# Shared experts on float16 parts, with the routed experts gathered into one stretch ahead of the last two chunks

## The reference, cut to what matters

```
logits = x @ gate_w.T                         # 32 experts in 8 groups, 3 groups kept, 6 experts per token
slot   = flat_e * 48 + pos                    # at most 48 slots per expert, the first tokens win
xb     = buf[:E * C].reshape(E, C, h)         # the slots' tokens
g, u   = split(xb @ w_gate_up)                # per expert, 176 + 176 columns
yb     = (silu(g) * u) @ w_down
out    = sum over the token's 6 slots of topk_w * yb
gs, us = split(x @ ws_gate_up)                # shared experts: all tokens, 352 + 352 columns
out    = out + (silu(gs) * us) @ ws_down
```

## Time and profile before

| what | us |
|---|---|
| median of 3 runs | 1727.3 (1720.38 to 1727.62) |
| the profiled execution | 1723.16 |
| its span, first to last instruction | 1721.3 |
| PE busy | 1472.5 (86%) |
| DVE busy | 1140.3 (66%) |
| ACT busy | 732.4 (43%) |
| POOL busy | 239.7 (14%) |
| mean granted clock of TensorE | 0.935 of full |

### The profile page before, as it was taken

How to read it: one execution, slowest core, us unless ns; L and a number is a source line. 1 busy time by engine, 2 the same in 40 slices (tenths; PEclk the granted TensorE clock), 3 DMA queues, 4 the chain that set the end, 5 groups by cost and what they waited for, 6 DMA issues and landing times.

```text
span 1721.3 us, 25882 instructions
## 1 busy us (share of the span) xinstructions
PE 1472.5 (86%) x9746; PEld 824.6 (48%) x9747; DVE 1140.3 (66%) x2283; ACT 732.4 (43%) x1232; POOL 239.7 (14%) x249
## 2 busy tenths in 40 slices
PE   4999999967989986568888898888988888998897
PEld 2666666644548876223344443343533344433355
DVE  5666666647421124688938779859879678789475
ACT  5455555511212220416755126754137752157630
POOL 3344444411330000100010000110000110000000
PEclk8999999987999988659999999999999998999998
DMA  2000000006014421232102012211023101113000
GB/s 112 14 26 25 24 24 24 24 13 195 15 40 128 151 76 63 64 61 44 32 10 40 1 37 44 44 28 34 1 44 56 44 19 25 34 27 45 31 1 25
DMA packets 137484, 75.23 MB, mean 44 GB/s; under 512 B 117648, under 2 KB 126352, under 8 KB 136592
## 3 DMA queue, kind: packets, MB, share of 16 engines
q1 hardware_dynamic: 136800, 72.02, 17.2%
q0 software_dynamic: 576, 1.77, 0.4%
HBM read 37.59 MB, written 9.06 MB: 27 GB/s over the span
## 4 chain that ended last, share of the span: by engine, by line
issue 57%; POOL 3%; DVE 0%; POOLq 0%; DVEq 0%
POOL rs_sb L1446 1%; POOL xs_sb L1452 1%; POOL ve_sb L1443 0%; POOL qks_sb L1466 0%; DVE bn_sb L1623 0%; DVE x_sb_sb L1656 0%; POOL v_sb L1464 0%; POOL qks_sb L1456 0%; POOLq L66 0%; POOLq L1159 0%; DVE mv_sb L1629 0%; DVEq L1159 0%; POOL v_sb L1463 0%; POOL qks_sb L1467 0%; DVE ident_h_sb L1839 0%
## 5 line engine op out<-in xcount | busy, mean ns | idle before, releaser
L1526 ACT ACTIVATE room_sb<-s_ps 128x1024 f32<-128x1024 f32 (+1 forms) x320 | 293.1, 940 | 176.1 <-PE s_ps L1998 172.2
L1707 DVE TENSOR_REDUCE mx_sb<-s_ps 128x1 f32<-128x512 f32 (+1 forms) x400 | 249.5, 650 | 60.3 <-PE s_ps L1974 37.7
L1971 PE MATMUL s_ps<-room_sb 48*128 48x512 f16 (+3 forms) x480 | 145.6, 340 | 33.8 <-DVE mx_sb L1702 21.3
L2018 PE MATMUL cm_ps<-room_sb,v_sb 128*32 128x512 f32 (+3 forms) x1536 | 157.0, 496 | 1.0 <-ACT room_sb L1532 0.8
L1998 PE MATMUL s_ps<-room_sb 51*128 51x128 f16 (+4 forms) x1152 | 136.6, 273 | 11.3 <-ACT room_sb L1526 7.9
L2124 PE MATMUL cm_ps<-w_fd_sb,room_sb 128*128 128x256 f32 x512 | 132.8, 409 | 12.6 <-DVE room_sb L1785 12.6
L1443 POOL TENSOR_TENSOR ve_sb<-mv_sb,eps_sb 128x4 f32<-128x4 f32 x24 | 5.3, 220 | 896.5 <-DVE mv_sb L1629 841.9
L396 DVE SCALAR_TENSOR_TENSOR x_sb_sb<-xp_sb,conv_w_sb,x_sb_sb 128x512 f32<-128x512 f32 x96 | 106.8, 1115 | 22.6 <-ACT x_sb_sb L319 20.5
L1971 PEld LDWEIGHTS s_ps<-room_sb 48*128 48x128 f16 x480 | 41.7, 94 | 155.2 <-DVE mx_sb L1707 79.4
L2124 PEld LDWEIGHTS cm_ps<-w_fd_sb,room_sb 128*128 128x128 f32 x512 | 98.3, 200 | 36.7 <-issue 14.0
L2111 PE MATMUL s_ps<-xbT_sb,w_fg_sb 128*128 128x512 f16 x384 | 102.0, 396 | 8.4 <-DVE ctok_sb L1755 7.7
(11 more groups left out here) (265 smaller groups left out, 2953.6 us busy)
## 6 DMA issues: line engine op xcount, KB each, us to landing
we_gu_sb<-we_gu SPq DMA_DIRECT2D x32, 352.0 KB
we_dn_sb<-we_dn SPq DMA_DIRECT2D x32, 176.0 KB
x_in_sb<-x SPq DMA_DIRECT2D x9, 512.0 KB, 3.6
rows<-x_sb_sb SPq DMA_DIRECT2D x8, 512.0 KB, 3.0
x_sb_sb<-rows SPq DMA_DIRECT2D x2, 2048.0 KB, 11.5
out<-x_sb_sb SPq DMA_DIRECT2D x8, 512.0 KB, 2.9
room_sb<-qks_sb SPq DMA_TRANSPOSE x88, 3.3
xp_sb<-w_in SPq DMA_DIRECT2D x1, 1024.0 KB, 5.5
```

What stands on the lines that cost most here:

```text
L1526: act.activation(weights[(g * NU + u) % SLOTS_P][:, 2 * pair:2 * pair + 2, 0:width(u) * P], W[s % 2][:, :, 0:width(u) * P], ACT.Exp, scale ...
L1707: dve.tensor_reduce(mx[:, pair, k % 2, slot:slot + 1], max_bank(g, m)[:, 0:count * P], AX.X, ALU.max, negate=True).then_inc(mx_ok, 1)
L1971: last = pe.matmul(bank[:, at * P:(at + plain) * P], query[head:head + NORM, i * P:(i + 1) * P], key[head:head + NORM, j * P:(j + plain) * ...
L2018: last = pe.matmul(O[32 * h:32 * h + 32, (i - half * GT) * P:(i - half * GT + count) * P], v[:, j, g * HG + h, :], weights[(g * NU + u) % ...
```

## The change

Five things, all of them in the first two parts of the program:

1. `conv_mlp_phase` splits the transposed result into two float16 parts, a high one by ACT from PSUM and a low one by POOL (which had copied float32). It also loads the shared experts' weights, on SP's queue in step 1, and splits them into two float16 parts in the last two steps. `experts_phase` then waits for no constants before its first chunk.
2. Each float32 product of the shared experts becomes three float16 products (high by high, low by high, high by low). The product of silu and up is made by DVE in all groups, in place, and split by ACT (high) and by POOL (low, groups 0 to 2) or DVE (low, from group 3).
3. A round is chunks 0 to 2, the four tiles of the group before, chunks 3 to 5. DVE's shared products are written in between the steps of the routing.
4. Counting moves to round 3, the slots' transposes to the last three turns of round 6 (eight in each), `gather` behind `add(3)`; all 32 experts stand in the first eight turns of round 7, four in each. The transposes of the slots' outputs follow, two in each of the two chunks and four tiles left, on two PSUM banks instead of four.
5. The slots' outputs and the one-hot matrices of the combination become float16 parts (they were float32r).

```diff
 # conv_mlp_phase
+                if n.reg is None and n.off == 1:
+                    for dst, src in zip(got_shared, ("ws_gu", "ws_dn")):
+                        sp.dma_start(dst[:], io[src]).then_inc(shared_ld, 16)
...
-                    wait(pool, xaT_ok, c(1, 1))
-                    pool.tensor_copy(xT[:, :, bass.ds(c(GTOK), GTOK)], xaT[:, :, :]).then_inc(xT_ok, 1)
+                    wait(pool, xTh_ok, c(1, 1))
+                    own = bass.ds(c(GTOK), GTOK)
+                    pool.tensor_tensor(xT[1][:, :, own], xaT[:, :, :], xT[0][:, :, own], ALU.subtract).then_inc(xT_ok, 1)
...
                     act.activation(xaT[:, :, :], tp[:, :, :], ACT.Copy).then_inc(xaT_ok, 1)
+                    act.activation(xT[0][:, :, bass.ds(c3(GTOK), GTOK)], tp[:, :, :], ACT.Copy).then_inc(xTh_ok, 1)
...
                     if has_c:
-                        wait(pe, xaT_ok, c3(1, 1))
+                        wait(pe, xTh_ok, c3(1, 1))
 # experts_phase
-COUNT_AT = 2
+COUNT_AT = 3
...
-SLOTS_AT = 5
-MOE_AT = 6
+SLOTS_AT = 6
+MOE_AT = 7
...
+EARLY = 3
+LATE = EARLY + GT
+TURNS = GT + 2 * NSX
+MOE_TURNS = LATE + 1
...
-        y = [sb(f"y{i}", [P, CJ, D], F32R) for i in range(2)]
+        y = [sb(f"y{i}", [P, CJ, D], F16) for i in range(2)]
...
         def experts_at(g, i):
-            n = (g - MOE_AT) * (GT + 2 * NSX) + i
-            return range(n * E // MOE_SLOTS, (n + 1) * E // MOE_SLOTS) if g >= MOE_AT else range(0)
+            return range(i * E // MOE_TURNS, (i + 1) * E // MOE_TURNS) if g == MOE_AT and i < MOE_TURNS else range(0)
+        def slots_at(g, i):
+            return range(8 * (i - LATE), 8 * (i - LATE) + 8) if g == SLOTS_AT and i >= LATE else range(0)
+        def outputs_at(g, i):
+            if g == MOE_AT:
+                return range(2 * (i - MOE_TURNS), 2 * (i - MOE_TURNS) + 2) if i >= MOE_TURNS else range(0)
+            return range(4 + 2 * (i - EARLY), 6 + 2 * (i - EARLY)) if g == NG else range(0)
+        def turns(g):
+            for i in range(TURNS):
+                chunk, tile = (i, None) if i < EARLY else (None, i - EARLY) if i < LATE else (i - GT, None)
+                if (chunk is not None and g < NG) or (tile is not None and g > 0):
+                    yield i, chunk, tile
 # POOL
             for g in range(1, NG):
                 if g < DVE_AT:
-                    act(g)
+                    act_low(g)
+                add(g - 1)
                 if g == GATHER_AT:
                     gather()
-                add(g - 1)
 # DVE
+            def product(g, i):
+                wait(dve, sg_ok, NSX * g + i + 1)
+                wait(dve, gu_mm, 2 * NSX * g + 2 * i + 2)
+                dve.scalar_tensor_tensor(sg[:, i, :], mm[(2 * i + 1) % 4][:, :], 1 / W_SCALE, sg[:, i, :],
+                                         ALU.mult, ALU.mult).then_inc(sa_ok, 1)
+            def low(g, i):
+                if g >= DVE_AT:
+                    wait(dve, sh_ok, NSX * g + i + 1)
+                    wait(dve, dn_mm, 2 * g)
+                    dve.tensor_tensor(su[1][:, i, :], sg[:, i, :], su[0][:, i, :], ALU.subtract).then_inc(sl_ok, 1)
+            product(0, 0)
             dve.memset(gm[:, :, EG:], LOW)
...
+            low(3, 0)
+            product(3, 1)
             dve.wait_ge(cnt_ok, 2)
             for i in range(2):
                 last = dve.max_index(at8[i][:, :], needle[:, i * (CJ - 8):i * (CJ - 8) + 8], cum[:, :])
+                if i == 0:
+                    low(3, 1)
+                    product(3, 2)
             last.then_inc(cnt_ok, 1)
+            low(3, 2)
+            product(4, 0)
 # PE
                 for k in range(KD):
-                    last = pe.matmul(mm[c % 4][:, :], ws_gu[:, k, col:col + P],
-                                     xT[:, k, g * GTOK:(g + 1) * GTOK], start=(k == 0), stop=(k == KD - 1))
+                    for wp, xp in PRODUCTS:
+                        last = pe.matmul(mm[c % 4][:, :], ws_gu[wp][:, k, col:col + P],
+                                         xT[xp][:, k, g * GTOK:(g + 1) * GTOK],
+                                         start=(k == 0 and wp == xp), stop=(k == KD - 1 and xp == 1))
...
             def down(g, t):
                 if t == 0:
-                    wait(pe, sa_ok, NSX * (g + 1))
+                    wait(pe, sl_ok, NSX * (g + 1))
...
-            pe.wait_ge(consts, 16 * N2)
...
+            def slot_out(j):
+                if j == 0:
+                    pe.wait_ge(ey_ok, E)
+                wait(pe, y_ok, j - 1)
                 for k in range(KD):
-                    last = pe.transpose(mm[j % 4][:, k * P:(k + 1) * P],
+                    last = pe.transpose(tp[j % 2][:, k * P:(k + 1) * P],
...
+            for g in range(NG + 1):
+                for i, c, t in turns(g):
+                    if c is not None:
+                        gate_up(g, c)
+                    if t is not None:
+                        down(g - 1, t)
...
+                        slot_features(m)
+                    experts(g, i)
+                    if (g, i) == (MOE_AT, MOE_TURNS - 1):
+                        expert_down(E - 1)
+                    for j in outputs_at(g, i):
+                        slot_out(j)
+                    if g == COUNT_AT and t == GT - 1:
+                        counted()
 # combination
-        hot = [sb(f"hot{i}", [P, CJ, P], F32R) for i in range(QUAD)]
+        hot = [sb(f"hot{i}", [P, CJ, P], F16) for i in range(QUAD)]
```

More of the change, by code:

```diff
@@ L355, in _ @@
                     squares(x1, ss2, ss2_ok)
+                if n.reg is None and n.off == NG:
+                    act.wait_ge(shared_ld, 32)
+                    for src, dst in zip(got_shared, shared):
+                        act.activation(dst[0][:, :, :], src[:, :, :], ACT.Copy, scale=W_SCALE).then_inc(wa_ok, 1)
         @block.vector
@@ L421, in _ @@
                     convolve(2)
+                if n.reg is None and n.off == NG + 1:
+                    for i, (src, dst) in enumerate(zip(got_shared, shared)):
+                        dve.wait_ge(wa_ok, 6 + i)
+                        dve.scalar_tensor_tensor(dst[1][:, :, :], src[:, :, :], W_SCALE, dst[0][:, :, :],
+                                                 ALU.mult, ALU.subtract).then_inc(wv_ok, 1)
+                    dve.wait_ge(wv_ok, 7)
                 if has_c:
@@ L831, in _ @@
             then(last)
+            product(0, 2)
             then(dve.memset(t8[:, :, TOPG:], LOW))
             for t in range(NT):
+                if t == NT // 2:
+                    product(1, 0)
                 last = dve.match_replace(gr[:, t, :], t8[:, t, :], gm[:, t, :], TAKEN)
@@ L845, in _ @@
             then(last)
-            dve.tensor_tensor(ex, sc[:, :, 0:E], t8b[:, :, 0:1].to_broadcast([P, NT, E]), ALU.subtract).then_inc(sub_ok, 1)
+            product(1, 2)
+            then(dve.tensor_tensor(ex, sc[:, :, 0:E], t8b[:, :, 0:1].to_broadcast([P, NT, E]), ALU.subtract))
+            assert step[0] == CENTERED
             then(dve.memset(t8b[:, :, TOPK:], LOW))
             for t in range(NT):
+                if t == NT // 2:
+                    product(2, 0)
                 last = dve.match_replace(sr[:, t, :], t8b[:, t, :], sc[:, t, :], TAKEN)
@@ L971, in down @@
                 if t == 0:
-                    wait(pe, sa_ok, NSX * (g + 1))
+                    wait(pe, sl_ok, NSX * (g + 1))
                     wait(pe, so_ok, 2 * g)
                 for k in range(NSX):
-                    last = pe.matmul(ro[t // 2][:, t % 2, :], su[:, k, t * P:(t + 1) * P], ws_dn[:, k, :],
-                                     start=(k == 0), stop=(k == NSX - 1))
+                    for ap, wp in PRODUCTS:
+                        last = pe.matmul(ro[t // 2][:, t % 2, :], su[ap][:, k, t * P:(t + 1) * P], ws_dn[wp][:, k, :],
+                                         start=(k == 0 and ap == wp), stop=(k == NSX - 1 and wp == 1))
                 if t % 2:
@@ L1011, in counted @@
             def counted():
+                pe.wait_ge(consts, 16 * N2)
                 pe.wait_ge(pre_ok, 8)
@@ L1053, in _ @@
                 last.then_inc(ty_ok, 1)
+            for g in range(NG + 1):
+                for i, c, t in turns(g):
+                    if c is not None:
+                        gate_up(g, c)
+                    if t is not None:
+                        down(g - 1, t)
+                    if g == SLOTS_AT and t == 0:
+                        pe.wait_ge(cnt_ok, 1)
+                        pe.wait_ge(cum_ok, NG)
+                        pe.matmul(tp[0][0:1, 0:NT], ones_f[:, 0:1], busy_f[:, :], start=True, stop=True).then_inc(busy_mm, 1)
+                    for m in slots_at(g, i):
+                        if m == 0:
+                            pe.wait_ge(busy_ok, 1)
+                            pe.wait_ge(gath, 16 * CJ)
+                        slot_features(m)
+                    experts(g, i)
+                    if (g, i) == (MOE_AT, MOE_TURNS - 1):
```

(9 more changed lines are left out.)

204 lines of the change are left out of this document (87 added, 117 removed).

## The result

| | before | after |
|---|---|---|
| median of 4 runs each, us | 1726.27 (1720.38 to 1727.62) | 1768.73 (1765.23 to 1773.32) |
| ratio, 95% interval | | 1.0256 [1.023, 1.0282] |
| profiled execution / its span, us | 1723.16 / 1721.3 | 1769.33 / 1767.5 |
| mean granted clock | 0.935 | 0.895 |
| PE busy, us | 1472.5 | 1502.0 |

What follows compares the result with a forecast made beforehand. PE, 95% busy in the routed experts, and its granted clock were taken to bound the kernel. 1723.2 + 40 (experts' block) - 2 (combination) = 1761 us, stated as 1759 for possible clock recoveries; range 1734 to 1775.

Steps and rivals of the forecast that it cites:

- rival A: The forecast itself: the low clock holds through the routed experts, four in a row; 1759 us, range 1745 to 1773; 74%.
- Rival D: Low clock as in rival A, but DVE's waits for chunks start the experts 10 to 15 us later; 1772 us; 5%.
- outputs to the block's end: Transposes of the slots' outputs behind the experts: 19 us, 14 at the full clock; block ends at 681 us.
- combination: Behind the experts' block, 192 products at 0.109 us, each quad waiting for one-hot matrices: between -5 and 0, taken as -2 us.
- The clock: In the experts' stretch: four experts in a row without shared work bring the granted clock to 0.5.
- The length: Experts' stretch: 4.5 us per expert at the low clock, 1.55 more than at full; 158 us, 156 with a full-clock start.
- The page that spoke the other way: Trainium skill's rule against long idle gaps between matmul bursts: half-microsecond gaps among the experts would keep the full clock.
- Rival B: The clock holds at the full level through four experts in a row; experts end at 604.5, total 1699 us; 12%.
- First part: `conv_mlp_phase`: ACT's extra copy and POOL's subtraction cost up to 0.2 us in seven steps, 1 us in all, within 0 to 7.
- Slots: Three turns with eight slot transposes each before the experts: 15 us, bounds 11 and 19; experts begin at 506.
- Routing: DVE's chain with shared products between its steps: starts at 401.9, casts end at 449.4, index at 465 us.
- a sign of being wrong: Experts beginning much before 495 or after 520 us, or a clock of 0.9 or more in their stretch.

Runs made afterwards that it cites:

- the kernel with the bank of its own: The kernel after, with the experts' second products in a PSUM bank of their own, so first products no longer wait for ACT's copy: 1725.75 us, ratio 1.0039.
- the last version: The kernel after with a bank for second products, two wide products per following expert, one before 22 slot transposes, POOL's additions of groups 2 to 6 held back: 1693.52 us.

## Why the prediction was right, step by step

The forecast came true in direction and range: 1768.7 us, slower, in 1734 to 1775. The mechanism is the one that rival A named, the low clock through the experts. The time itself lies 10 us above A's 1759 and 3 below D's 1772, since the start was late as D had it. The main size, 159 us for 156, came out of two errors that cancel. Most other terms came out longer than the prediction had them.

| step | predicted | measured | off by |
|---|---|---|---|
| chunk / tile at the full clock, start to start, us | 1.30 / 0.98 | 1.30 / 0.99 | |
| first chunk, at | 396 | 399.7 | +3.7 |
| index, at | 465 | 469.5 | +4.5 |
| down(3) ends, at | 467.5 | 472.3 | +4.8 |
| slots' turns begin, at | 491 | 497.3 | +6.3 |
| experts' first turn, at | 506 | 517.25 | +11.3 |
| an expert at the low clock, us | 4.5 | 4.77 | +0.27 |
| experts' stretch, from that turn's chunk, us | 156 | 159 | +3 |
| outputs to the block's end, us | 19 | 17.7 | -1.3 |
| combination, us | -2 | -3.6 | -1.6 |

- *The clock.* Right in level. That the order is enough for it, the run of the kernel before in rows of four shows; whether it is all of it is open, since the kernel after with its experts spread, most of them still in pairs, got 0.63 only. My reason for it, that PE did little but expert products, was half of it: narrow products, put into the waits, hold the clock too, and why they do is open.
- *The length.* An expert cost 4.77 us at the low level, not 4.5; by the prediction's own sum that makes 166.5 us of the stretch, not 158. The clock came back twice for some 3.2 us, which gave 6.5 back, and 159 is what was left. That these two nearly cancel is luck. The price of the low level was mis-sized twice: the two experts of the earlier trace rows lie 2.83 us apart (its rows do not show the 2.97), so it is 4.77 - 2.83 = 1.94 us for each expert and not 1.55.
- *The page that spoke the other way.* Rival B rested on full clock through gaps of half a microsecond. The gaps did matter (filled, they give B's clock in most executions, and a stretch of 92.6 us where B had 99.5), but they are short, and that section of the Trainium skill ("TensorE: Matmul & The Clock Gate", "Why this matters for your kernels") warns of long ones. The measurement decides: 0.52 with gaps of 0.51 us, and a fall at 584.5 us with no gap at all in the kernel with the bank of its own.
- *First part.* Six of the seven steps cost nothing: from one normalization to the next 42.36 us after, 42.34 before. The last one, beside which the weights are split, took 1.5 us more (43.10 against 41.58). The first normalization stands 3.07 us later (92.46 against 89.39 us), ahead of any step; another execution with the same first part has it at 88.46 and its first chunk at 395.94, as forecast. So most of the 3.7 us is one execution's start, not the change.
- *Slots.* Predicted 15 us with bounds of 11 and 19, measured 19.9. Mis-sized for two reasons: the low part that waits beside POOL's addition (1.74 us, in which PE stood idle for DVE), and a clock that fell there already, at 501.5 us; the next two chunks took 2.4 to 2.8 us. The fall came behind this wait, but without the addition it came too.
- *Routing.* The index came 0.8 us later than the late start explains. The prefix sums took 7.05 us, where they had taken 5 x 0.69 and I had counted no change. POOL's additions account for 2.0 us of that (5.03 without them); the rest stands beside POOL's low part, which no run took away.
- *Rival D.* The start was 10 to 15 us late as D had it, but for another reason than the counting of DVE's waits that D gave: start-up, POOL beside DVE and the early fall of the clock. The first expert began at 519.81 us, just inside the 520 that the prediction had named as a sign of being wrong.

The sum by the profile: 693.9 - 640.6 = 53.3 us at the block's end, 3.6 us back in the combination, and 3.5 us less from there to the end of the span, where nothing was changed (1037.5 us against 1040.9; another execution with the same last part has 1032.3). Together 46.2 us, the difference of the spans. The forecast had 40 and -2: it was 13 us short at the block's end, and 5 us that came back behind it, 3.5 of them by chance, hid a part of that.

## What to carry to other kernels

Where small products stand in a row, read the granted clock of that stretch before counting what a reordering saves: here moving wide products out from between the experts cost more than the shorter products gave back. A short wait in such a row can be worth filling with products that nobody needs, if an idle PSUM bank is there. When a wait is taken away, look for the next one: here it was the weights' loads. And an operation of DVE with two operands in SBUF should not be timed to stand beside POOL's.

## What the runs showed of the hardware that was not expected

- Added work made the kernel 55 us faster in the median: 48 products more, 1768.7 to 1713.4 us, with one of ten executions at 1771.6.
- With the bank of its own PE was busy without a gap from 566.2 to 584.5 us and had the low clock in that time from 567.5 to 581.1, and again from 584.5. With narrow products in the waits it was as busy for 95 us and kept 1.0 throughout.
- Executions of one kernel can differ by their clock: with the bank of its own and nothing added the ten go from 1717 to 1741 us, at mean clocks of 0.925 to 0.906, and with two products in each wait from 1699 to 1772, at 0.943 to 0.898. The five of the last version go from 1691 to 1698 and the four of the kernel before in rows of four from 1785 to 1788.
- One POOL addition of 2.35 us beside a DVE operation of 0.69 us stretched it to 2.43; it ended 0.55 us behind the addition.
